# A graph network on one core: the area reserved for GpSimd's transfer descriptors is 8192 bytes per partition in place of 16384

## What is computed

```
edge_index = stack([src, dst])                     # dst sorted, 206250 edges
L0: agg = segment_sum(x[src], dst); x@w_self.T + b + (agg/deg)@w_neigh.T + b'
L1: h = relu([x[src], edge_attr] @ W1 + b1) @ W2 + b2; agg = scatter_mean(h, dst)
    relu([x, agg, u[0]] @ W3 + b3) @ W4 + b4
L2: e = segment_sum(edge_attr @ We + be, dst); c = [x, e]; h = c + segment_sum(c[src], dst)
    relu(h @ W1 + b1) @ W2 + b2
L3: graph attention with 4 heads of 32: h = x @ W, softmax over the edges of each dst of
    leaky(a_src[src] + a_dst[dst]), out = segment_sum(h[src] * alpha, dst), norm, relu
x = layernorm(x + L(x)) after each layer
```

## Time and profile before

| | us |
|---|---|
| median of 3 runs | 6218.11 |
| lowest and highest run | 6216.2, 6225.41 |
| profiled execution, its own time | 6181.86 |
| its span | 6180.0 |

### The profile page before, as it was taken

How to read it: one execution, slowest core, us unless ns; L and a number is a source line. 1 busy time by engine, 2 the same in 40 slices (tenths; PEclk the granted TensorE clock), 3 DMA queues, 4 the chain that set the end, 5 groups by cost and what they waited for, 6 DMA issues and landing times.

```text
span 6180.0 us, 70833 instructions
## 1 busy us (share of the span) xinstructions
PE 4521.5 (73%) x24017; PEld 3636.4 (59%) x24017; DVE 2509.1 (41%) x8563; ACT 1745.2 (28%) x3903; POOL 3125.5 (51%) x3324
## 2 busy tenths in 40 slices
PE   6999978889899899998998997234443444434445
PEld 5888865666666666666668996234343443434434
DVE  8999952333333333333335443123222222222324
ACT  5888841222222222222224553001110111101111
POOL 0000026666666666666650002666666666666664
PEclk9999989999999999999999998566666656666666
DMA  6777765555555555555546885222222222222221
GB/s 153 163 164 166 165 161 180 181 180 182 184 179 182 177 183 178 180 184 177 182 152 196 243 243 156 47 48 50 49 48 50 48 49 50 50 48 49 50 49 34
DMA packets 472464, 804.79 MB, mean 130 GB/s; under 512 B 72608, under 2 KB 301131, under 8 KB 462123
## 3 DMA queue, kind: packets, MB, share of 16 engines
q0 software_dynamic: 140192, 443.73, 28.9%
q1 hardware_dynamic: 317802, 346.76, 17.7%
q10 hardware_dynamic: 14112, 9.74, 0.5%
HBM read 663.72 MB, written 136.22 MB: 129 GB/s over the span
## 4 chain that ended last, share of the span: by engine, by line
PE 54%; another core or an unknown queue 24%; issue 9%; DVE 9%; DMA 2%; ACT 1%; POOL 0%; DVEq 0%; ACTq 0%; SPq 0%
PE bank L1028 17%; PE bank L1015 12%; PE bank L1197 7%; PE bank L682 5%; PE bank L662 2%; DVE ring L1335 2%; DMA atab<-at 2%; PE bank L1548 2%; PE bank L583 1%; DVE hs L631 1%; PE bank L964 1%; DVE hs L629 1%; DVE tops L1285 1%; PE bank L1528 0%
## 5 line engine op out<-in xcount | busy, mean ns | idle before, releaser
L543 POOL DMA_INDIRECT ring<-ptab,src x1612 | 1526.6, 947 | 829.4 <-issue 446.2
L543 POOL DMA_INDIRECT ring<-htab,src x1612 | 1539.4, 955 | 772.4 <-issue 465.4
L1028 PE MATMUL bank<-ring,oh 128*126 128x384 f32 x3224 | 1280.0, 509 | 80.8 <-issue 76.9
L981 DVE TENSOR_TENSOR ring<-bank,ring 128x512 f32<-128x512 f32 x806 | 540.3, 687 | 1588.6 <-remote 715.7
L1548 PE MATMUL bank<-ring,oh 128*126 128x132 f32 x3224 | 689.0, 348 | 552.4 <-issue 546.4
L1015 PE MATMUL bank<-w1e,ea 128*128 128x256 f32 x3224 | 896.8, 397 | 117.4 <-issue 89.0
L1548 PEld LDWEIGHTS bank<-ring,oh 128*126 128x126 f32 x3224 | 593.8, 249 | 622.4 <-issue 611.2
L1015 PEld LDWEIGHTS bank<-w1e,ea 128*128 128x128 f32 x3224 | 627.6, 198 | 393.1 <-issue 167.7
L1028 PEld LDWEIGHTS bank<-ring,oh 128*126 128x126 f32 x3224 | 624.4, 197 | 361.5 <-issue 155.6
L997 ACT ACTIVATE ring<-ring 128x1024 f32<-128x1024 f32 x403 | 425.4, 1056 | 1224.4 <-DVE ring L981 875.1
L682 PE MATMUL bank<-xhl,at 128*126 128x258 f32 x3822 | 712.4, 323 | 0.0
(11 more groups left out here) (271 smaller groups left out, 4466.9 us busy)
## 6 DMA issues: line engine op xcount, KB each, us to landing
atab<-at POOLq DMA_DIRECT2D x78, 1543.5 KB, 9.9
ring<-ea_r SPq DMA_DIRECT2D x403, 256.0 KB
ea<-ea_t SPq DMA_DIRECT2D x403, 256.0 KB
adjb<-atab SPq DMA_DIRECT2D x156, 535.5 KB, 4.7
adjb<-atab SPq DMA_DIRECT2D x78, 472.5 KB, 4.4
ring<-ptab,src POOLq DMA_INDIRECT x1612
ring<-htab,src POOLq DMA_INDIRECT x1612
ptab<-pO ACTq DMA_DIRECT2D x49, 128.0 KB, 7.3
```

Of the source, the lines that this page charges most:

```text
L543: return e.indirect_dma_start(o, None, table, bass.IndirectOffsetOnAxis(ap=src[:, t:t + 1], axis=0))
L981: e.tensor_tensor(group1(gi, m % 2), MLP[m % NM][:, :].rearrange("p (g f) -> p g f", g=2), group1(gi, m % 2), ALU.add).then_inc(s_edge, 1)
L1028: w = e.matmul(SUM[s % 2][0:SL, 0:384], slots_of(s, i), rv1[:, t // G % NR1, t % G, :], start=i == 0, stop=t == END[s])
```

## The change

The program object is built with `dynamic_dma_scratch_size=8192`. The reserved area for the descriptors of GpSimd's transfers is half as large, and all the kernel's tensors in SBUF start 8192 bytes lower in their partitions. No instruction, wait, buffer or order is changed, and the space that comes free is used by nothing.

```diff
-    nc = bacc.Bacc("TRN2", target_bir_lowering=False, num_devices=1)
+    nc = bacc.Bacc("TRN2", target_bir_lowering=False, num_devices=1, dynamic_dma_scratch_size=8192)
```

## The result

The changed kernel takes 6231.13 us (median of 15 runs, 6222.81 to 6241.88), the kernel before 6216.47 us (15 runs beside them, 6212.54 to 6225.41): a ratio of 1.0021, 95% interval 1.0014 to 1.0028. It is slower by 0.21%, 14.7 us between the medians and 13.0 us above the forecast of 6218.1 us, and the interval excludes no change. The time lies inside the predicted range. "Within 0.2%", on which 0.92 was set, was missed by the least margin.

A forecast was written before the change was run, and what follows sets the result against it. It took TensorE to bound stages 0 to 2, stage 3 unexplained but not paced by GpSimd. All terms were 0, so the profiled 6181.86 us plus 36.25 us to the runs' median gave 6218.1 us, range 6206 to 6232 us.

The forecast's parts named there:

- (a): Whole kernel: the instruction stream is the same, with no instruction, wait or DMA added, removed or moved; cost 0.
- (b): All tensors lie 8192 bytes lower in their partitions: cost 0, bounded by run scatter at -2 to +7 us.
- (c): GpSimd's gathers, stages 1 and 3: half the area holds 56, filled 57 times in place of 28; cost 0.
- bound of 2.58 us for a filling: GpSimd's gathers: the most one filling of the area could cost, a wait for everything under way to land.
- the one pause of 1.29 us: Stage 1, before the 114th gather: GpSimd's idle time of 1.59 us less the normal 0.30, read as the area first full.
- part (d): Stage 0's stores: about 18 fit the area now and 9 after, one or two are under way; cost 0.
- 1.2 us that the sum left: GpSimd's "issue" idle time of 911.6 us in 2985 pieces, less 910.4 us at 0.305 us each.
- Rival A: Whole kernel: no change, also if size has no effect but the address shift has; 6218 us, chance 0.93.
- Rival B: Stages 1 and 3: GpSimd's pauses at each filling reach the path, 74 us (6292 us) or 148 us (6366 us); chance 0.04.
- C: Stage 3: places come free only with consumption of rows, limiting how far GpSimd runs ahead; 683 us, 6901 us; chance 0.01.
- D: Faster: pause at the 114th gather gone, or addresses or smaller area suit the DMA engines better; 1.29 us, 0.02%; chance 0.02.

The follow-up runs named there:

- e18: The changed kernel again, against the kernel before at 6188.85 us: ratio 1.0012 [1.0003, 1.0020].
- e17: Descriptor area of 8192 bytes, padded so all addresses stay, against the kernel before at 6188.85 us: ratio 1.0011 [1.0002, 1.0020].
- e13: The changed kernel again, against the kernel before at 6187.93 us: ratio 1.0014 [1.0005, 1.0023].
- e14: Descriptor area of 8192 bytes, padded so all addresses stay, against the kernel before at 6187.93 us: ratio 1.0011 [1.0002, 1.0020].
- e15: Descriptor area of 2048 bytes, padded so all addresses stay, against the kernel before at 6188.85 us: ratio 0.9999 [0.9990, 1.0008].
- e1: The kernel before with its area of 16384 bytes written out, against the kernel before at 5569 us: ratio 0.9999 [0.9990, 1.0008].
- e5: Descriptor area of 1024 bytes, padded so all addresses stay, against the kernel before at 5573 us: ratio 1.0779 [1.0764, 1.0794].
- e16: Descriptor area of 4096 bytes, padded so all addresses stay, against the kernel before at 6188.85 us: ratio 1.0032 [1.0019, 1.0045].
- e12: The kernel before with its area of 16384 bytes written out, against the kernel before at 6187.93 us: ratio 1.0001 [0.9992, 1.0010].
- e7: The changed kernel again, against the kernel before at 5573 us: ratio 1.0004 [0.9995, 1.0013].

## Why the prediction was wrong

The time lies in the range only because the range left 14 us for scatter; its mechanism, no effect at all, was wrong where the result was taken.

(a), the instruction stream, held: both profiles count 70833 instructions, with 1612 + 1612 gathers and 78 stores.

(b), the addresses at 0, held as far as it was measured: e18 is 0.0001 above e17 and e13 0.0003 above e14, both inside their intervals. An effect of the addresses of up to about 0.1% is not excluded, since each interval is as wide as that to either side.

(c) is the step that failed, in one of its terms and in its conclusion. What held: the area's size in gathers (7 at 1024 bytes, and e15's pauses fit 14), a filling costs GpSimd nothing as long as the transfers whose place is wanted have landed, and slot waits absorb pauses (e15, 110 us for nothing). The bound of 2.58 us for a filling held for all but one of the pauses put down to "issue": the pauses shown at 1024 and 2048 bytes cost 1.9 to 2.0 us each above the usual 0.30, the longest at 2048 bytes 3.2 us. My reason was incomplete, though. It is not the age of the transfer whose place is wanted that counts but the age of the newest one on its semaphore: with 2048 bytes the wanted place was 14 x 1.25 = 17.5 us old and GpSimd still paused.

What failed: I took the one pause of 1.29 us as what an area that is full for the first time costs, and forecast that it would move to the 57th gather. It didn't move, it went. It stands at the 114th gather in both profiles with 16384 bytes of the 6190 kind and not in e1, which has the same area. Why it stands there is open. It is hidden, and is not the 0.21%. Two things could have been seen beforehand. By part (d) the area fits 18 stores, so the 78 stores of stage 0 had filled it four times before the first gather, and the 114th gather can't be the first to find it full unless the count starts anew with stage 1. And the 1.2 us that the sum left for this pause are within its rounding (0.305 us is known to about 0.0005, which makes 1.4 us in 2985 pieces); the profile has a second gap, of 0.67 us at 2654.14 us. That the count of 113 read off from it fits the 7 gathers of e5 is luck as far as this reading goes.

And the conclusion: I summed what GpSimd loses and found 0, rightly, and from that put the whole change at 0: pauses would "move nothing behind them". Stage 1 did get longer, by 7 us, with TensorE idle for 252 to 260 us in place of 249: 2353.75 us is the stage on average of e13, e14, e17 and e18, against 2346.35 of the two with 16384 bytes. Of the 6 to 10 us that the medians of these four lie above the kernel before, that is the larger part. The term of the sum that should have stood there is +7 us with a bound of about +20 (what 4096 bytes gave), in place of 0. On the occasion of the result it was 15 us; since the profile of before is not typical of its runs there, I can't split these by stage.

Rival A, no change, is refuted for the occasions of the result's kind. At 5570 us it holds to within 0.05%, though five of the six ratios with 8192 bytes lie above 1, at 1.0003 to 1.0005, each with an interval that takes in 1. Rival B was the right side and the wrong mechanism: no row of the changed kernel shows pauses at every filling, and where GpSimd paces the kernel, with B's condition met in full, the changed kernel takes 1.0000 to 1.0004 of the time. At 6190 us e15 speaks against its coupling: 110 us of pauses at GpSimd left the time as it was. C is refuted by how far POOL ran ahead. With places for 56 gathers the changed kernel, and with places for 28 e16, still issued 105 gathers in stage 3 before the first slot wait, at the 106th, as the kernel before did; the 106th in the timeline of POOL, of the changed kernel and then of e16:

```profile
4005.98 0.94 POOL L543 DMA_INDIRECT ring<-htab,src  x1 [16.37 <-remote]
```

```profile
3991.47 0.94 POOL L544 DMA_INDIRECT ring<-htab,src  x1 [16.15 <-remote]
```

For D nothing spoke. What was wrong with 0.92 for "same" is that it came from one engine's account, while in stage 1 the chain put 9.2% on "issue" and PE was idle for 249 of 2347 us, which I had not explained. A forecast of the sign would have had no ground either: 2048 bytes give none of it.

**What stays open** is how the size of the area reaches TensorE. Ruled out are pauses at GpSimd (none over 0.4 us in the profile after; in e13, e14, e16, e17 and e18 two to four of over 0.6 us, together at most 5.5 us, and in e12 three, together 4.1 us), the gathers' own time (946 to 947 ns in each of these profiles in stage 1), a late landing (DVE and ACT wait for two or three each), and a monotone effect of the size. The effect shows only on the occasions on which gathers don't pace stage 1. That alone may be why: at 5570 us a delay of 7 us at TensorE could hide behind the gathers, so these runs don't tell whether it exists there. Those occasions are also the ones with "issue" idle time of PE at L1548, where 5570 us has none. But that idle time doesn't follow the effect: 520 us in e12, 471 to 519 us in the four with 8192 bytes, 603 us in e16, 362 us in e15, which costs nothing, and 723 us in the changed kernel's first profile; and it stands in stage 3, while the 7 us stand in stage 1. That a small change in when gathers are issued shifts TensorE's idle time is an argument, not a finding; no run here makes it larger or smaller by itself.

## What to carry to other kernels

The area for the descriptors of GpSimd's transfers can be small at no price at GpSimd, as long as it holds more transfers than are issued one after another on one semaphore. Here, with groups of 21 on one semaphore, a gather every 1.25 us and a landing of 2.6 us, 28 places brought no pause at 5570 us and three at 6190 us, as many as the control with 113 places; 14 brought one a group, hidden by slot waits in the one set in which it ran; and 7 cost 7.8%, nearly all of which went when the landings were spread over four semaphores. Between 14 and 28 nothing was measured. The time can still move by 0.1 to 0.3% in ways that no row explains. An account that shows that an engine loses nothing doesn't prove that the time is the same, and a forecast of "no change" to within 0.2% needs the unexplained idle time of the pacing engine in its range. Test such a change on more than one occasion: here three of six would have called it free.

## What the runs showed of the hardware

The same kernel took 5568 and 6188 us under one chip number, with spans at a mean granted TensorE clock of 0.875 and 0.829. The clock alone isn't the difference. Stage 1 of e7, of the 5570 us kind, in the columns of the earlier trace rows:

```profile
873.30:2889.40 2016.10, 1956.80 (x8037) 1397.97 (x8038) 757.96 (x1550) 524.91 (x752) 1525.30 (x1612) 1.00 0.68 210
```

Beside the kernel before (2347.4 us, TensorE busy for 2098 us at a granted clock of 0.94) TensorE is busy for 141 us less at a clock of 1.00, but the stage is 331 us shorter; the other 190 us are idle time. In the longer kind TensorE also begins its instructions in stage 3 with gaps that nothing shown explains; the timeline of PE of the kernel before:

```profile
5005.38 0.62 PE L1520 MATMUL bank<-wide,ohT 126*128 126x168 f32 x1 [0.30 <-issue]
5008.15 0.38 PE L1548 MATMUL bank<-ring,oh 128*126 128x132 f32 x1 [2.15 <-issue]
5009.55 0.38 PE L1548 MATMUL bank<-ring,oh 128*126 128x132 f32 x1 [1.02 <-issue]
```

So which engine paced this kernel was a matter of the occasion: GpSimd in stages 1 and 3 at 5570 us, where gathers stand back to back in both; at 6190 us not GpSimd but, in stage 1, TensorE with its idle time, and in stage 3 something that no row names. A profile tells it for its own occasion alone.
